# Strip loads, block statistics and leading maxima put in another order in a four-layer cross-attention and expert kernel

## The reference, cut to what matters

```python
x = x + L0_xattn(layernorm(x), ctx)      # A0
x = x + L0_ffn(layernorm(x))             # F0: int8 weights, int16 activations
x = x + L1_xattn(layernorm(x), ctx)      # A1
x = x + L1_ffn(layernorm(x))             # F1: 8 experts, top 2, and a shared one
x = x + L2_xattn(layernorm(x), ctx, mask)        # A2
x = x + L2_ffn(layernorm(x))             # AS (self-attention), then F2: 8 gated experts, top 2
x = x + L3_xattn(ctx, ctx, layernorm(x), mask)   # A3
x = x + L3_ffn(layernorm(x))             # F3: 8 experts, top 2, layernorm of the result
# each attention, per head:
attn = softmax(q @ k.T * scale)          # scores, maximum, exponential, sum
ctx_out = attn @ v
```

## Time and profile before

| | us |
|---|---|
| runs, lowest to highest | 1792.71 to 1793.48 |
| median | 1792.91 |
| the profiled execution, as timed | 1801.7 |
| its span in the profile | 1799.9 |
| PE busy | 1690.6 (94%) |
| DVE busy | 1119.9 (62%) |
| ACT busy | 1071.3 (60%) |
| POOL busy | 637.2 (35%) |

### The profile page before, as it was taken

One profiled execution on the slowest core, in us unless ns is written; L12 is line 12 of the kernel. 1 busy time (PEld: TensorE's weight loads), 2 busy tenths in 40 slices (PEclk: granted clock), 3 DMA queues, 4 the chain that ended last, 5 costly groups with the idle time before them and its releaser, 6 DMA issues.

```text
span 1799.9 us, 38537 instructions
## 1 busy us (share of the span) xinstructions
PE 1690.6 (94%) x14287; PEld 1133.4 (63%) x14322; DVE 1119.9 (62%) x3293; ACT 1071.3 (60%) x2147; POOL 637.2 (35%) x1050
## 2 busy tenths in 40 slices
PE   7999978999999999999999999989998999999998
PEld 3555545455568988854444455568885555489997
DVE  5788958888832232357777676646667888633332
ACT  2788852888864444447777755443335888744443
POOL 4454333344332223223444443223353454222221
PEclk9999988899999999979999999989998999999999
DMA  5344203455200000213332244300032654000000
GB/s 169 122 136 147 76 24 96 131 176 154 74 7 1 1 1 19 77 59 95 108 89 87 60 137 123 90 1 1 1 105 65 184 162 121 13 1 7 7 7 7
DMA packets 114852, 132.35 MB, mean 74 GB/s; under 512 B 14934, under 2 KB 78700, under 8 KB 114668
## 3 DMA queue, kind: packets, MB, share of 16 engines
q1 hardware_dynamic: 114668, 129.90, 23.8%
HBM read 83.45 MB, written 46.40 MB: 72 GB/s over the span
## 4 chain that ended last, share of the span: by engine, by line
PE 79%; ACT 9%; DVE 5%; issue 4%; POOL 2%; DMA 1%; SPq 0%; POOLq 0%; DVEq 0%; ACTq 0%
PE ps_s L1424 16%; PE ps_av L1280 14%; PE ps_s L1237 11%; PE ps_t L1400 10%; ACT prob L986 6%; PE ps_t L1253 4%; PE ps_s L1400 4%; PE ps_t L1264 3%; PE ps_m L1327 2%; PE ps_m L1336 2%; PE ps_m L1321 2%; PE ps_m L1314 1%; PE ps_m L1289 1%; PE ps_m L1349 1%; PE ps_t L1266 1%
## 5 line engine op out<-in xcount | busy, mean ns | idle before, releaser
L986 ACT ACTIVATE prob<-ps_t 128x512 f32<-128x512 f32 (+1 forms) x1152 | 616.1, 588 | 188.4 <-PE ps_t L1253 182.2
L1716 DVE TENSOR_REDUCE mx<-ps_s 128x1 f32<-128x512 f32 x752 | 474.2, 683 | 83.0 <-PE ps_s L1237 81.3
L1237 PE MATMUL ps_s<-kst,qst 32*128 32x512 f32 (+2 forms) x1248 | 382.4, 486 | 16.9 <-DVE mx L1716 8.7
L1253 PE MATMUL ps_t<-qmx,kst 32*128 32x256 f32 (+1 forms) x2304 | 333.9, 341 | 23.2 <-ACT prob L986 20.3
L1424 PEld LDWEIGHTS ps_s<-w_ffn,prob 128*128 128x128 f32 x2688 | 317.8, 194 | 10.6 <-issue 3.4
L1424 PE MATMUL ps_s<-w_ffn,prob 128*128 128x128 f32 x2688 | 324.4, 278 | 0.0
L1280 PE MATMUL ps_av<-prob,vaug 128*32 128x256 f32 (+1 forms) x4608 | 311.0, 389 | 3.2 <-ACT avs L1027 3.2
L1237 PEld LDWEIGHTS ps_s<-kst,qst 32*128 32x128 f32 x1248 | 166.4, 190 | 176.8 <-issue 96.6
L1173 ACT ACTIVATE prob<-ps_t,b1c 128x512 f32<-128x512 f32 x204 | 125.5, 686 | 238.6 <-PE ps_t L1400 238.6
L2006 DVE SCALAR_TENSOR_TENSOR acc<-ps_s,comb,acc 128x128 f32<-128x128 f32 x336 | 94.6, 345 | 259.1 <-PE ps_s L1424 259.1
L1253 PEld LDWEIGHTS ps_t<-qmx,kst 32*128 32x128 f32 x2304 | 201.9, 190 | 61.1 <-ACT prob L986 52.2
(11 more groups left out here) (240 smaller groups left out, 2258.6 us busy)
## 6 DMA issues: line engine op xcount, KB each, us to landing
kst<-k_parts SPq DMA_DIRECT2D x128, 256.0 KB, 3.5
qst<-q_parts SPq DMA_DIRECT2D x160, 128.0 KB, 3.6
k_parts<-k_hi SPq DMA_DIRECT2D x64, 256.0 KB, 3.0
q_parts<-q_hi SPq DMA_DIRECT2D x80, 128.0 KB, 2.4
ctxT<-in_ctxT SPq DMA_DIRECT2D x32, 256.0 KB, 2.7
k_parts<-k_lo SPq DMA_DIRECT2D x32, 256.0 KB, 3.1
q_parts<-q_lo SPq DMA_DIRECT2D x40, 128.0 KB, 2.4
w_ffn<-in_F_w SPq DMA_DIRECT2D x18, 256.0 KB, 2.9
```

The costliest lines, as they stand in the source:

```text
L986: nc.scalar.activation(row[:, S * kt:S * kt + w], ps_t[TURN[unit(ph, g, n) % 8]][:, 0:w], ACT.Exp).then_inc(sig["exp_done"], 1)
L1237: pe.matmul(dst, qst[p][strip, g, q * 128:(q + 1) * 128], kst[p][strip, g, 0:nk], start=True, stop=True).then_inc(sig["s_ready"], 1)
L1253: mm = pe.matmul(dst, kst[p][strip, g, kt * 128:(kt + 1) * 128], qmx[strip, g % 2, seen(ph, kt):], start=not opened, stop=not opened or c ...
L1716: dve.tensor_reduce(mx[:, buf, i:i + 1], src, AX.X, ALU.max, negate=True).then_inc(sig["max_done"], 1)
```

## The change

Three places are changed.

1. `load_strips`: the four loads of keys are issued as soon as the keys are saved, ahead of the wait for the saved queries; the four loads of queries follow together. This holds for every batch of every attention phase.
2. F0 to A1: TensorE makes the query product of A1's batch 0 directly behind the turn of its tokens, after output 3. VectorE takes the statistics of the last block's two halves (`new_statistics` of block 3) behind the first 16 maxima of A1, and POOL its two powers of them behind the second split of maxima.
3. F2 to A3: "MT" stands in the middle of expert 7, where pair 6 stood; pairs 6 and 7 are taken by TensorE behind the second product of expert 7, and by VectorE behind the accumulation of expert 7 and ahead of `result` (new tokens and their statistics).

```diff
--- before.py
+++ after.py
@@ -77,9 +77,9 @@
            (6, "mid"): 3, (6, "end"): 4, (7, "mid"): 5, (7, "end"): 6, (8, "mid"): "MT", (8, "end"): 7},
     "F2": {(0, "mid"): "K0", (0, "end"): "XT0", (1, "mid"): "Q0", (1, "end"): "V0", (2, "mid"): "B0", (2, "end"): "K1",
            (3, "mid"): "XT1", (3, "end"): "Q1", (4, "mid"): 0, (4, "end"): 1, (5, "mid"): 2, (5, "end"): 3,
-           (6, "mid"): 4, (6, "end"): 5, (7, "mid"): 6, (7, "end"): "MT"},
+           (6, "mid"): 4, (6, "end"): 5, (7, "mid"): "MT"},
 }
-LED_PAIRS = {"A2": 8, "A3": 7}
+LED_PAIRS = {"A2": 8, "A3": 6}
 CT_AT = 3
 BIAS_BEHIND = 4
 LED = {"A1": "F0", "A2": "F1", "A3": "F2"}
@@ -573,9 +573,10 @@
                 if ph == "A3":
                     sp.wait_ge(mask_saved[p], 32 * (bt.half + 1))
                 sp.wait_ge(k_saved[p], saved(ph, bt))
+                for g in range(NG):
+                    sp.dma_start(kst[p][:, g, 0:nk].bitcast(F32), scratch["k"][p][128 * g:128 * (g + 1), 0:nk]).then_inc(stacked[p][g], 16)
                 sp.wait_ge(q_saved[p], saved(ph, bt))
                 for g in range(NG):
-                    sp.dma_start(kst[p][:, g, 0:nk].bitcast(F32), scratch["k"][p][128 * g:128 * (g + 1), 0:nk]).then_inc(stacked[p][g], 16)
                     sp.dma_start(qst[p][:, g, :].bitcast(F32), scratch["q"][p][128 * g:128 * (g + 1), :]).then_inc(stacked[p][g], 16)
 
             def first_contexts(ph):
@@ -814,6 +815,9 @@
                         split_maxima(ph, b0, 0)
                         add_queries(ph, b0, 0)
                     split_maxima(ph, b0, 1)
+                    if ph == "A1":
+                        for half in range(2):
+                            power("F0", NBLK - 1, half, (NBLK - 1) * TB + half * QT, QT)
                 elif ph == "A0":
                     split_k(ph, b0)
                     split_q(ph, b0)
@@ -966,7 +970,7 @@
                     power(ph, 0, 1, QT, QT)
                     normalise_batch("A1", b1)
                     split_q("A1", b1)
-                    for blk in range(1, NBLK):
+                    for blk in range(1, NBLK - 1):
                         for half in range(2):
                             power(ph, blk, half, blk * TB + half * QT, QT)
                 else:
@@ -1578,9 +1582,9 @@
 
                 for n in range(2 * NBLK):
                     output(n // 2, n % 2)
-                    what = {3: ("XT", 0), 4: ("Q", 0)}.get(n)
-                    if what:
-                        misc(what[0], "A1", Batch(what[1]))
+                    if n == 3:
+                        misc("XT", "A1", Batch(0))
+                        misc("Q", "A1", Batch(0))
                 for what in ("XT", "Q"):
                     misc(what, "A1", Batch(1))
 
@@ -1797,16 +1801,16 @@
 
             def attention(ph):
                 b0 = Batch(0)
-                if ph in ("A2", "A3"):
-                    for pair in range(LED_PAIRS[ph], 8):
-                        lead(ph, pair)
-                elif ph == "A0":
+                if ph == "A0":
                     quantise_weights()
                     output_bias(ph)
                 if ph in ("A0", "A1"):
                     for g in range(2):
                         for i in range(8):
                             maximum(ph, b0, g, i)
+                if ph == "A1":
+                    new_statistics(NBLK - 1, 0)
+                    new_statistics(NBLK - 1, 1)
 
                 def body(bt, first, last):
                     pph, pbt = preceding(ph, bt, 1)
@@ -1859,6 +1863,11 @@
                 link(dve.tensor_scalar(dst, src, scale, ROUND, ALU.mult, ALU.add))
                 return dve.tensor_scalar(dst, dst, ROUND, A16, ALU.subtract, ALU.min)
 
+            def new_statistics(blk, half):
+                wait(dve, "x_new", cnt.at("x_new", "F0", blk, half))
+                n = 2 * blk + half
+                all_statistics([x_tok[:, QT * n + q, :] for q in range(QT)], QT * n)
+
             def quantised_ffn():
                 ph = "F0"
                 link.until(since["inner"])
@@ -1899,11 +1908,6 @@
                     dst = x_tok[:, QT * n:QT * (n + 1), :]
                     dve.scalar_tensor_tensor(out=dst, in0=ps_o[n % 4][:, 0:S].rearrange("p (q d) -> p q d", q=QT), scalar=svec[:, 5:6],
                                              in1=dst, op0=ALU.mult, op1=ALU.add).then_inc(sig["x_new"], 1)
-
-                def new_statistics(blk, half):
-                    wait(dve, "x_new", cnt.at("x_new", ph, blk, half))
-                    n = 2 * blk + half
-                    all_statistics([x_tok[:, QT * n + q, :] for q in range(QT)], QT * n)
 
                 def first_tokens():
                     wait(dve, "rstd_done", cnt.at("rstd_done", ph, 0, 0))
@@ -1945,8 +1949,6 @@
                 new_statistics(2, 0)
                 new_statistics(2, 1)
                 add(3, 1)
-                new_statistics(3, 0)
-                new_statistics(3, 1)
 
             def experts(ph):
                 ne = 9 if ph == "F1" else 8
@@ -2050,6 +2052,9 @@
                             lead({"F1": "A2", "F2": "A3"}[ph], LEADS[ph].get((e, "end")))
                         if not last and e == 3:
                             norm(ph, blk + 1)
+                    if last and ph == "F2":
+                        for pair in range(LED_PAIRS["A3"], 8):
+                            lead("A3", pair)
                     result(blk, E if ph != "F2" else E - 1)
 
                 for blk in range(NBLK - 1):
```

## The result

| | before | after |
|---|---|---|
| first comparison: median (lowest to highest), us | 1792.81 (1792.69 to 1793.48) | 1818.72 (1810.31 to 1836.29) |
| ratio, 95% interval | | 1.0137 [1.0094, 1.0181] |
| the same kernel again, in a later comparison | 1796.73 (1787.09 to 1805.07) | 1812.35 (1798.11 to 1837.46) |
| ratio, 95% interval | | 1.0078 [1.0050, 1.0107] |
| the profiled execution: span | 1799.9 | 1808.5 |

The change makes the kernel slower, by 0.8 to 1.4%. The forecast, 1793.9 in a range to 1798.0, was wrong in size: +1.0 us, where 25.9 and 15.6 were measured. That it, too, said slower was luck, since its +1.0 came from places that did not bring the loss. Runs of one kernel lay farther apart in the later comparisons than in the first, so a ratio is only read inside its own comparison. Ratios are taken from each kernel's runs within 1.5% of its fastest.

What follows compares the result with a forecast made beforehand. TensorE was taken as the main bound, holding 79% of the chain against DMA's 1%. The openings' 0.7 − 0.2 + 0.5 = +1.0 us, added to 1792.9, gave 1793.9 us, range 1787.5 to 1798.

Steps and rivals of the forecast that it cites:

- The step that failed: Batches other than the openings: loads wanted some ten microseconds after issue, so the reordering was taken to cost or gain nothing.
- The diff therefore has three places: Claim that the change can matter only at the openings of A0, A1 and A3.
- A0's opening: Keys' loads ahead of the first query load: issue gains 0.3 us, landing comes later; net +0.7 us, ends −0.3 and +1.5.
- My three rates: A0's opening: load rates 0.25 MB per us, 323 and 403 GB/s, for queries landing at 22.0, 21.3 or 20.7; 323 taken.
- A1's opening: Earlier query product brings first maximum 0.9 us sooner, moved statistics spend it; net −0.2 us, ends −0.5 and +0.9.
- A3's opening: TensorE starts 0.9 us sooner, but VectorE's group 2 maxima come 0.7 later; net +0.5 us, ends −0.9 and +0.8.
- Openings at full clock: Faster rival: A1's and A3's openings both keep 2.4 GHz, saving 6.4 us, giving 1787.5; chance 0.21.
- Later return of the clock: Slower rival: full clock returns 3.5 us later in all three openings, +4.7 us, giving 1798.6; chance 0.19.
- Keys don't delay queries: Rival: A0's opening gives −0.3 and A1's stays bound by VectorE, giving 1792.9; chance 0.1.
- The three parts' sum: Openings of A0, A1 and A3 together: 0.7 − 0.2 + 0.5 = +1.0 us.

Runs made afterwards that it cites:

- e2: The changed kernel with its loads back in the old alternating order in every phase; ratio 1.0002 to the kernel before.
- e4: The kernel before with all four key loads ahead of the queries in AS (self-attention) alone; ratio 1.0059.
- e8: The kernel before with only the F2 to A3 part of the change; ratio 1.0017.
- e14: The kernel before, in AS alone with key and query loads alternating but group 0's pair last; ratio 1.0215.
- e15: The kernel before, in AS alone with group 0's pair first, then keys 1 to 3, then queries 1 to 3; ratio 1.0002.
- e7: The kernel before with only the F0 to A1 part of the change; ratio 1.0036.
- e10: The kernel before, in AS alone with the four query loads ahead of the wait for the keys and their four loads; ratio 1.0018.
- e11: The kernel before, in AS alone with four key loads, then queries 1, 2, 3 and group 0's queries last; ratio 1.0234.
- e13: The kernel before, in AS alone with group 0's query load fifth and no burst of keys ahead of queries; ratio 1.0087.
- e16: The kernel before with four key loads ahead of the wait for the queries in the cross-attentions alone, not in AS; ratio 1.0005.
- e5: The changed kernel, in AS alone with group 0's pair first, then keys 1 to 3, then queries 1 to 3; ratio 1.0027 to the kernel before.
- e9: The changed kernel measured again unaltered in a later comparison; median 1812.35 us, ratio 1.0078 to the kernel before.

## Why the prediction was wrong

**The step that failed**: "In every other batch the loads are wanted some ten microseconds after they are issued; that cover hides both signs." It rested on the earlier trace rows: no wait in 38 of 40 batches. A wait of zero says that the slack is not negative; how large it is stands elsewhere, in the distance from the landing to the instruction that reads. In AS, from its second batch on, the load of group 0's queries was wanted 3.7 to 4.6 us after its issue and 1.1 to 2.1 us after its landing, in the batch above 1.3, and the edit's own delay there, three more issues of 0.47, is 1.4. (Behind the two openings, no batch of the cross-attentions had less than 1.8.) "The diff therefore has three places" was wrong: it has a fourth, run through seven times. The second half of the miss is that I priced the low clock only where it already was, at the openings, and not where a new stop could bring it. By the estimate above that is the larger part: 12 of 13.6 us in the profile.

**A0's opening** (+0.7, ends −0.3 and +1.5). Chain of the kernel after, answering to the earlier trace rows:

```profile
15.58 0.53 SPq L577
...
17.59 4.29 DMA qst<-q_parts
...
22.76 4.28 DVE mx L1720 x7
```

The keys' loads went out when foretold (15.6), the query load too (17.6 for 17.7), and it landed at 21.88. My three rates gave 22.0, 21.3 and 20.7: the slowest, 0.25 MB per us from the landings, was right, and I had taken the middle one. First maximum +1.34 here, and 1.49 to 2.80 in the five other profiles with this opening. The ring order that the Trainium skill states (DMA: Bandwidth & Descriptors, "Queues, rings and completion order") agrees with what was measured: megabyte ahead, one or two microseconds late; one load ahead, early by one. What follows in the first batch can't be read from one profile. Value products (timeline of TensorE in A0, after; compare):

```profile
49.23 1.07 PE L1284 MATMUL ps_av<-prob,vaug 128*32 128x256 f32 x16
...
57.48 1.07 PE L1284 MATMUL ps_av<-prob,vaug 128*32 128x256 f32 x16
```

Full speed at 49 us already, where it was half at 59 before. The first batch, from its first maximum on, is 3.2 us shorter, and kernels that leave this opening untouched do that too (e2, e4, e8, e14, e15: −2.6 to −4.2; e7, e10, e11, e13: 0 to −0.6). It belongs to the execution, not to the change.

**A1's opening** (−0.2, ends −0.5 and +0.9). Timelines of the kernel after, answering to the earlier trace rows (ACT, PE) and the earlier trace rows (DVE):

```profile
287.46 0.38 ACT L1004 ACTIVATE xnT<-ps_m 128x256 f32<-128x256 f32 x1 [13.80 <-PE ps_m L1313]
```

```profile
296.58 0.67 PE L1318 MATMUL ps_m<-xnT,w_A 128*128 128x256 f32 x2 [0.57 <-ACT xnT L1004]
298.34 0.50 PE L1241 MATMUL ps_s<-kst,qst 32*128 32x512 f32 x3 [1.09 <-DMA qst<-q_parts]
```

```profile
298.92 4.88 DVE L1720 TENSOR_REDUCE mx<-ps_s 128x1 f32<-128x512 f32 x8 [1.98 <-PE ps_s L1241]
304.21 5.11 DVE L1720 TENSOR_REDUCE mx<-ps_s 128x1 f32<-128x512 f32 x8 [0.42 <-PE ps_s L1241]
309.24 0.48 DVE L1656 BATCH_NORM_STATS2 st<-x_tok 128x6 f32<-128x128 f32 x2
...
310.57 3.05 DVE L1720 TENSOR_REDUCE mx<-ps_s 128x1 f32<-128x512 f32 x5
```

The whole frame lies 3.0 us earlier. The mechanism is as foretold: the statistics stand behind 16 maxima and take 1.33 us, and the next maximum follows without an idle. But the first maximum gained 0.16 us and not 0.9. The keys' loads went out at 291.58, in the frame of before 294.6, where I had 294.4; the first score then waited until 298.34, that is 301.35 where I had 300.2 to 300.3. It is again the loads' rate: megabyte ahead, the queries came more than a microsecond late. The net, to the tokens of the first batch, is −0.81 in the profile after. Seven kernels that leave this opening alone lie there at −0.37 to −0.93, so the profile before was itself slow here (23.9 us of low clock in this batch, 20 to 21 in nearly all others), and the four with this part and no four keys ahead lie at −0.23 to −0.56. The part saved nothing that these runs show; the sign may be the other one, some 0.4 us.

**A3's opening** (+0.5, ends −0.9 and +0.8). Timelines of the kernel after, answering to the earlier trace rows:

```profile
1371.01 1.13 DVE L2008 SCALAR_TENSOR_TENSOR acc<-ps_s,comb,acc 128x128 f32<-128x128 f32 x4 [3.77 <-PE ps_s L1428]
...
1376.52 5.07 DVE L1720 TENSOR_REDUCE mx<-ps_s 128x1 f32<-128x512 f32 x8
```

```profile
1374.16 0.53 PE L1241 MATMUL ps_s<-kst,qst 32*128 32x512 f32 x1 [0.21 <-DVE mx L1720]
```

```profile
1377.01 1.04 POOL L706 TENSOR_TENSOR rstd<-veps,neg_half 128x4 f32<-128x4 f32 x1
```

The mechanism is as foretold, its size 0.3 too large. From VectorE's last sum to group 2's maxima it was 4.76 us and is 5.51: +0.75 where my steps made it 1.0; and the second product came 0.5 sooner where I had 0.25. The eight profiles with this part have the last block's tokens 1.8 to 2.0 us later and the first batch shorter by nearly as much: net +0.1 to +0.27. Kernels without it lie at 0 to +0.4 in the same sum (e7 at +3.9), so the net cost can't be told from none. TensorE's 2.8 us idle is gone and buys nothing, as said.

**The rivals.** Openings at full clock: in no profile. In the first batch of A1 the low clock took 20 to 24 us in 17 of the 18 profiles, in that of A3 13 to 15 in 17. Later return of the clock: twice, without regard to the change, in A1 of the second profile of the changed kernel (44 us, and that batch 7.6 us longer) and in A3 of e7 (24 us). "Keys don't delay queries" is refuted by A0. The three parts' sum, +1.0, can't be told from what they brought: e16 with all openings' loads at 1.0005 and e2 with the rest at 1.0002. The 16 to 26 us came from where the prediction had no step.

## What to carry to other kernels

Where an edit holds for a loop of many batches, read the smallest slack in every phase that runs through it, as the distance from landing (or end) to first use, and not the list of waits; zero waited says nothing on how near it was. A load that somebody will want first goes first in the queue: each issue put ahead of it costs its issue time (0.47 us here) and its bytes. And where TensorE is the bound, price a stop of a microsecond or two by the low clock that may follow, not by its length: in e14 stops of 6.2 us went with a time 38 us longer.

## What the runs showed of the hardware

- The granted clock can stay at 0.50 while TensorE is busy 99% of the time, for 26 to 37 us in e14; what ends such a stretch no row told. It can also fall without a stop. In e5 no idle of TensorE over 0.31 us stands in the ten microseconds before 1109 (windows, columns as in the earlier trace rows):

```profile
1100.00:1109.00 9.00, 7.94 (x80) 4.30 (x79) 5.84 (x38) 5.02 (x13) 4.10 (x11) 1.00 0.33 89
1110.00:1143.00 33.00, 32.67 (x198) 17.95 (x190) 15.27 (x83) 10.36 (x25) 7.20 (x17) 0.50 0.33 97
```

- Nor does every stop bring it: of eighteen stops in AS of 0.3 us and more, in after, e4, e9, e11, e13 and e14, ten had the clock fall within 2.6 us, eight had not, the two of e13's profile among them.
- SyncE's issue of one load takes 0.32 to 0.6 us, most often 0.43 (0.47 with the gap to the next), and now and then over a microsecond (1.09 in the row of the kernel before above); four in a row took 1.75 to 2.72. The Trainium skill (DMA: Bandwidth & Descriptors, "Anatomy of one DMA — SWDGE (gpsimd) path") has, for the path from GpSimd, that many descriptors can be emitted before their cost shows. That path is not used here; on SyncE's queue the cost showed with each load: three loads ahead were 1.4 us.
- Executions of the kernel before ranged from 1786 to 1823 us where runs were many, and one took 2052 at a mean clock of 0.742. Part of it is how long AS runs at the low clock: in the seven profiles of kernels that leave AS as it was, the stretch took 188.7 to 195.8 us, with 11 to 31 us at the low clock.
